# A graph attention and mixture-of-experts stack: second-layer probabilities of three target chunks made together

## The reference, cut to what matters

```
x = x + gat0(layernorm(x), adj)      # 4 heads, softmax over neighbours
x = x + moe0(layernorm(x))           # 8 experts, hidden 512, top 2
x = x + gat1(layernorm(x), adj)      # one attention matrix, see below
x = x + moe1(layernorm(x))           # 2 layers of 256x256, one of 16 experts for each run of 32 rows

gat1:  Wh = x @ W.T ; s1, s2 = score of each row and head
       z[i,j,h] = s1[i,h] + s2[j,h] ; e[i,j] = mean_h max(z, 0.2 z)
       attn = softmax(where(adj > 0, e, -inf)) ; out = attn @ Wh
```

## Time and profile before

| what | value |
|---|---|
| median of 3 runs | 751.7 us (750.96 to 751.88) |
| the profiled execution's own time | 748.28 us |
| its span, first to last instruction | 746.2 us |
| PE, DVE, ACT, POOL busy | 616.9, 532.2, 388.3, 225.4 us |
| mean granted TensorE clock | 0.903 of 2.4 GHz |
| expert weights by the SP queue (L362) | 128 transfers of 256 KB |

### The profile page before, as it was taken

One profiled execution on the slowest core, in us unless ns is written; L12 is line 12 of the kernel. 1 busy time (PEld: TensorE's weight loads), 2 busy tenths in 40 slices (PEclk: granted clock), 3 DMA queues, 4 the chain that ended last, 5 costly groups with the idle time before them and its releaser, 6 DMA issues.

```text
span 746.2 us, 14828 instructions
## 1 busy us (share of the span) xinstructions
PE 616.9 (83%) x5288; PEld 468.8 (63%) x5288; DVE 532.2 (71%) x1050; ACT 388.3 (52%) x761; POOL 225.4 (30%) x151
## 2 busy tenths in 40 slices
PE   2765466999999999989999969995479969879696
PEld 1554355687776877758777645775446737647463
DVE  6569998876687756857566289459597999998300
ACT  1876569377875778837887546541013223222231
...
DMA packets 30704, 63.09 MB, mean 85 GB/s; under 512 B 4557, under 2 KB 7637, under 8 KB 30645
## 3 DMA queue, kind: packets, MB, share of 16 engines
...
...
## 4 chain that ended last, share of the span: by engine, by line
PE 64%; DVE 17%; ACT 8%; issue 5%; POOL 3%; DMA 1%; SPq 1%; DVEq 0%; ACTq 0%
PE bank L604 16%; PE bank L616 12%; PE bank L564 10%; PE bank L687 6%; PE bank L549 5%; PE bank L724 4%; PE bank L717 3%; ACT arena L964 3%; DVE arena L1218 2%; DVE arena L1206 2%; POOL reg_b L461 2%; DVE reg_c L1360 2%; DVE arena L1214 2%; PE bank L540 1%; ACT ysb L921 1%
## 5 line engine op out<-in xcount | busy, mean ns | idle before, releaser
L454 POOL TENSOR_TENSOR x<-x,ysb 128x512 f32<-128x512 f32 x36 | 62.3, 1730 | 308.5 <-ACT ysb L921 304.2
L964 ACT ACTIVATE arena<-sbc,nd 128x512 bf16<-128x512 f32 x204 | 130.4, 718 | 37.1 <-PE bank L564 37.1
L616 PEld LDWEIGHTS bank<-arena,reg_c 128*128 128x128 f32 x1024 | 116.8, 192 | 7.2 <-issue 7.2
L604 PE MATMUL bank<-hTc,arena 128*128 128x512 f32 x256 | 120.9, 628 | 0.0
L564 PE MATMUL bank<-reg_b,arena 128*128 128x99 bf16 x2048 | 103.9, 214 | 19.6 <-DVE arena L1218 19.6
L616 PE MATMUL bank<-arena,reg_c 128*128 128x128 f32 x1024 | 116.9, 275 | 0.0
L564 PEld LDWEIGHTS bank<-reg_b,arena 128*128 128x128 bf16 x2048 | 101.4, 102 | 23.2 <-issue 11.4
L911 ACT ACTIVATE reg_c<-bank,b 128x512 f32<-128x512 f32 x128 | 87.9, 687 | 36.3 <-PE bank L604 36.3
L1206 DVE TENSOR_TENSOR arena<-maskT,arena 128x2048 bf16<-128x2048 bf16 x48 | 65.9, 1372 | 48.2 <-ACT arena L964 48.0
L1218 DVE TENSOR_TENSOR arena<-maskT,arena 128x2048 bf16<-128x2048 bf16 x64 | 95.6, 1493 | 2.2
L1360 DVE SCALAR_TENSOR_TENSOR reg_c<-reg_b,nd,reg_c 128x512 f32<-128x512 f32 x144 | 96.4, 743 | 0.0
(11 more groups left out here) (170 smaller groups left out, 795.9 us busy)
## 6 DMA issues: line engine op xcount, KB each, us to landing
arena<-in_wrT SPq DMA_DIRECT2D x128, 256.0 KB, 3.0
...
```

Source lines behind the costliest of these rows:

```text
L454: nc.gpsimd.tensor_tensor(xi, xi, ysb[:, e % 3, :].rearrange("p (t d) -> p t d", d=P), ALU.add).then_inc(s_acc, 1)
L604: mm(bank[b][:, :], w1[:, s, e % 2, c * P:(c + 1) * P], hTc[:, :], start=True, stop=True).then_inc(full[b], 1)
L616: last = mm(bank[b][:, i * P:(i + 1) * P], hid[:, e % 2, c, i * P:(i + 1) * P], w2[:, s, e % 2, c, :], start=(c == 0), stop=(c == HC - 1))
L964: last = af(ind[:, q, 1, j, :], sbc[:, h, :], ACT.Relu, bias=nd[:, q * QT + j, h:h + 1], scale=BIG)
```

## The change

The second attention no longer goes chunk by chunk. Target chunks 0, 1 and 2 are made together: one product covers WW = 1536 columns (`wide`, four slots), source tiles go in pairs (`wide_pair`, 8 products), and `attend_wide` sums a pair with 24 matmuls of 129 columns into banks 0 to 3. Five of the eight pairs are put beside the mixture of chunk 3, which keeps to banks 4 (outputs) and 5, 6, 7 (hidden blocks, HT). VectorE runs the five in a row, held only by the slots (`s_widef`: pair g waits until PE has summed pair g-2), then waits for all of GpSimd's adds of chunk 3, normalises it, and runs the other three. Chunk 3's own probabilities stay in products of 512 columns (`last_tiles`), and `attend1` sums them inside the second mixture of chunks 0, 1 and 2: 2 calls before it, then 2, 4 and 8.

For that, chunk 0 is prepared before the gate scores of chunk 3 and chunks 1 and 2 soon after, each with its source rows; the values are scaled on ScalarE (`scale_values`) instead of GpSimd; the score bounds (`nmx`) are worked out early, ahead of the first indicators; the score rows of chunk 3 go into `hT` and `ysb`, `v1` shares the buffer of `sbc`, and htt and hn of the second mixture (`tiles1`) move into the arena. The SP queue starts the selected weights after the last `attend_wide` (`full[3]`) and the scaled values. The extra indicators and source rows past the last chunk are gone, and all hardware loops but SP's are written out. `layer`, `turn`, `hidden` and `output` are as before, and so is the last chunk of the second mixture.

```diff
+WT = 3 * CT
+WW = WT * P
...
         odiv = sb("odiv", [P, CT, P])
-        sbc = sb("sbc", [P, H, CW])
+        heads = sb("heads", [P, T * (P + 1)])
+        sbc = heads[:, 0:H * CW].rearrange("p (h i) -> p h i", h=H)
+        v1 = heads[:, :].rearrange("p (t v) -> p t v", t=T)
         att = sb("att", [P, CT * 2 * VW])
...
-        whx1 = arena[:, 0:T * XM].rearrange("p (t k) -> p t k", t=T)
-        prob0 = arena[:, 4096:8192].rearrange("p (s i) -> p s i", s=8)
+        whx1 = arena[:, 0:2 * CT * XM].rearrange("p (s t k) -> p s t k", s=2, t=CT)
+        wide = arena[:, 2048:2048 + 4 * WW].rearrange("p (s i) -> p s i", s=4)
         wsel = arena[:, 0:8192].rearrange("p (s k n) -> p s k n", s=2 * L * GT, k=KC)
         at = [8192]
...
         u6 = u.rearrange("p (t h b) s v -> p t h b s v", t=T, h=H)
-        v1 = reg_b[:, 0:T * (P + 1)].rearrange("p (t v) -> p t v", t=T)
-        rows1 = reg_b[:, T * (P + 1):T * (P + 1) + 2 * H * CW]
+        rows1 = reg_b[:, 0:H * WW].rearrange("p (h i) -> p h i", h=H)
+        rows3 = [hT[:, h * CW:(h + 1) * CW] for h in range(H - 1)] + [ysb[:, 1, :]]
...
-        BANK5 = C * (E0 // 2 + 1)
+        HT = (5, 6, 7)
+        BANK3 = C + (C - 1) * E0 + 1
+        BANK5 = (C - 1) * (E0 // 2 + 1) + len(range(0, E0 * HC, len(HT))) + C
...
-                    load_pair(c, h, True)
+                    if c == C - 1 and h >= 2:
+                        sp.wait_ge(ev["y"], c * (E0 + 1) + (2 if h == 2 else 5))
+                    load_pair(c, h, c < C - 1 or h < 2)
...
-            sp.wait_ge(s_u, H + C)
-            sp.wait_ge(s_exp, 2 + C)
+            sp.wait_ge(s_v1, C)
+            sp.wait_ge(full[3], BANK3)
...
-                if c == C - 1 and e in (2, 3, 5, E0):
-                    g = (2, 3, 5, E0).index(e)
-                    tiles = slice(g * CT, (g + 1) * CT)
-                    pool.wait_ge(s_exp, 3 + g)
-                    nc.gpsimd.tensor_tensor(v1[:, tiles, 0:P], whx1[:, tiles, 0:P],
-                                            v1[:, tiles, P:P + 1].to_broadcast([P, CT, P]),
-                                            ALU.mult).then_inc(s_u, 1)
...
+            for c in range(1, C):
+                chunk0(c)
...
+            def attend_wide(g):
+                if g == 0:
+                    for b in range(WT // 3):
+                        use(b, "att")
+                pe.wait_ge(s_v1, g // 2 + 1)
+                for t in (2 * g, 2 * g + 1):
+                    pe.wait_ge(s_wide, t + 1)
+                    for i in range(WT):
+                        b, o = i // 3, i % 3 * (P + 1)
+                        last = mm(bank[b][:, o:o + P + 1], wide[:, t % 4, i * P:(i + 1) * P], v1[:, t, :],
+                                  start=(t == 0 and i % 3 == 0), stop=(t == T - 1), skip_group_check=True)
+                        if t == T - 1 and i % 3 == 2:
+                            last.then_inc(full[b], 1)
+                if g < T // 2 - 2:
+                    last.then_inc(s_widef, 1)
...
+            def first(e):
+                if e % 2 == 0:
+                    pe.wait_ge(s_wp[e // 2 % 2], k.event(f"pair{e // 2 % 2}", 32))
+                for c in range(HC):
+                    b = HT[(e * HC + c) % len(HT)]
+                    use(b, "hid")
+                    mm(bank[b][:, :], w1[:, e // 2 % 2, e % 2, c * P:(c + 1) * P], hTc[:, :], start=True,
+                       stop=True).then_inc(full[b], 1)
+            def second(e):
+                use(4, "y")
+                pe.wait_ge(ev["hid"], (C - 1) * E0 * HC + (e + 1) * HC)
+                for i in range(CT):
+                    for c in range(HC):
+                        last = mm(bank[4][:, i * P:(i + 1) * P], hid[:, e % 2, c, i * P:(i + 1) * P],
+                                  w2[:, e // 2 % 2, e % 2, c, :], start=(c == 0), stop=(c == HC - 1))
+                last.then_inc(full[4], 1)
...
+            prepare1(0)
+            source_rows1(0)
+            scores(odiv)
+            first(0)
+            first(1)
+            prepare1(1)
+            prepare1(2)
+            second(0)
+            source_rows1(1)
+            source_rows1(2)
+            first(2)
+            second(1)
+            combine(4)
+            first(3)
+            second(2)
+            first(4)
+            second(3)
+            attend_wide(0)
+            first(5)
+            second(4)
+            attend_wide(1)
+            first(6)
+            second(5)
+            attend_wide(2)
+            first(7)
+            second(6)
+            attend_wide(3)
+            second(7)
+            attend_wide(4)
             prepare1(3)
-            for q in range(2, Q):
-                quad(q)
+            source_rows1(3)
+            for g in range(5, T // 2):
+                attend_wide(g)
+            attend1(0)
+            attend1(1)
...
-                            for h in range(H):
-                                source_row(h, next_rows)
+                        for t in products.get((i, l), ()):
...
+                        for t in products.get((i, l), ()):
+                            attend1(t)
                         turn(i)
...
+            expert_chunk(odiv, {(1, 0): (2,), (2, 0): (3,)})
+            expert_chunk(xn, {(0, 0): (4,), (1, 0): (5,), (2, 0): (6,), (3, 0): (7,)})
+            expert_chunk(odiv, {(0, 0): (8,), (0, 1): (9,), (1, 0): (10,), (1, 1): (11,), (2, 0): (12,),
+                                (2, 1): (13,), (3, 0): (14,), (3, 1): (15,)})
...
+            def scale_values(c):
+                act.wait_ge(s_exp, 3 + c)
+                for i in range(CT):
+                    t = c * CT + i
+                    last = af(v1[:, t, 0:P], whx1[:, c % 2, i, 0:P], ACT.Copy, scale=v1[:, t, P:P + 1])
+                last.then_inc(s_v1, 1)
...
+            scale_values(0)
+            first(0)
+            gate()
+            first(1)
+            prepare1(1)
+            prepare1(2)
+            second_layer(0, 4)
+            source_rows1(1)
+            source_rows1(2)
+            scale_values(1)
+            scale_values(2)
+            first(2)
+            second_layer(1, 4)
+            combine(4)
+            for e in range(3, E0):
+                first(e)
+                second_layer(e - 1, 4)
+            second_layer(E0 - 1, 4)
             prepare1(3)
-            sums(3 * (P + 1), P + 1)
+            source_rows1(3)
+            scale_values(3)
+            sums(*[3 * (P + 1)] * (WT // 3), to=reg_b)
...
+            then(v.tensor_tensor(wnorm[:, 0:H], wnorm[:, 0:H], wnorm[:, H:2 * H], ALU.max))
...
+            replicate(1)
+            dve.wait_ge(s_acc, E0 + 1)
+            norm(0, 2 * C - 1)
             merge(C - 1, H - 1)
-            norm(C - 1, 2 * C - 1)
+            norm(C - 1, C, odiv)
+            dve.wait_ge(s_acc, (C - 1) * (E0 + 1))
+            statistics(CT)
+            then(statistics(2 * CT, CT))
+            deviations(2 * CT)
+            dve.wait_ge(ev["hTc"], 2 * C)
+            scale(CT, xn, 0)
             best(C - 1, 2 * C - 1)
+            dve.wait_ge(ev["hTc"], 2 * C + 1)
+            scale(2 * CT, odiv, CT)
             gate(C - 1, 2 * C - 1)
...
+            def products(h, tiles, slots, row, columns, ready):
+                before = k.at("step") - len(tiles)
+                for j, t in enumerate(tiles):
+                    p = slots[:, t % slots.shape[1], :]
+                    if h:
+                        dve.wait_ge(s_step, before + j + 1)
+                    last = v.scalar_tensor_tensor(p, row, nd[:, t, h:h + 1], p if h else maskT[:, t, columns],
+                                                  ALU.max, ALU.mult)
+                    last.then_inc(s_step if h < H - 1 else ready, 1)
+                if h < H - 1:
+                    k.event("step", len(tiles))
+            def wide_pair(g):
+                dve.wait_ge(s_exp, 3 + g // 2)
+                if g >= 2:
+                    dve.wait_ge(s_widef, g - 1)
+                for h in range(H):
+                    products(h, (2 * g, 2 * g + 1), wide, rows1[:, h, :], slice(0, WW), s_wide)
+            def last_tiles(first, n):
+                if first >= 8:
+                    dve.wait_ge(s_probf, first // QT - 1)
+                for h in range(H):
+                    products(h, range(first, first + n), prob, rows3[h], slice(WW, N), s_prob)
+            def merge1(t0, n, at, src):
+                a3 = src[:, 0:(at + n) * (P + 1)].rearrange("p (t v) -> p t v", v=P + 1)
+                for i in range(n):
+                    xo = x[:, t0 + i, :]
+                    last = v.scalar_tensor_tensor(xo, a3[:, at + i, 0:P], rden[:, at + i:at + i + 1], xo, ALU.mult,
+                                                  ALU.add)
+                return last
+            def divisors(n, src):
+                a3 = src[:, 0:n * (P + 1)].rearrange("p (t v) -> p t v", v=P + 1)
+                then(v.reciprocal(rden[:, 0:n], a3[:, 0:n, P]))
```

(26 more changed lines are left out.)

287 lines of the change are left out of this document (77 added, 210 removed).

## The result

The changed kernel takes **754.6 us** (median of 6 runs, 754.1 to 757.5) against 751.4 of the kernel before in the same comparison: 1.0051 of its time, with a 95% interval of 1.0032 to 1.0069. It is slower, by a little; the forecast of 750.4 had it 0.2% faster. The profiled execution has a span of 752.2 us (746.2 before).

What follows compares the result with a forecast made beforehand. Bounds by stretch: TensorE in chunk 3's mixture and the last chunk, VectorE's products between, both in the second mixture. 581.9 to W plus 163 gave span 744.9; adding 2.1 and 3.4 gave 750.4 us, range 739 to 764.

Steps and rivals of the forecast that it cites:

- W: Point where the last `attend_wide` is done: forecast at T + 135.6 = 581.9 us, with 163 us following to the end.
- The product of 1536 columns: VectorE's wide product: 1.73 us each, from a line through two measured sizes; a pair of tiles 13.8 us.
- Rival 4: Wide products save nothing, at 1.99 us each: 17 us, total 767; chance 0.03.
- T: Point where the twelfth score row is ready, ahead of the wide pairs: forecast at 446.3 us.
- GpSimd is kept out for the whole run: Beside VectorE's runs of products, a GpSimd add waits until the run ends: waits of 9.75, 16.44 and 22.07 us.
- rival 2: Wide products don't keep GpSimd out: pairs end at T + 71.8, W 10 us earlier, total 740.4; chance 0.12.
- The gap of 2.1 us: VectorE's wait for `attend_wide(0)` after two pairs; three GpSimd adds wait there, and the third was taken to get in.
- rival 1: GpSimd's third add misses VectorE's gap, so chunk 3 is normalised 10 us later, at T + 98: total 760; chance 0.27.
- GpSimd's adds have four outputs of slack: In the second mixture, behind W, VectorE's narrow products beside GpSimd's adds were taken to cost nothing.
- The weights: Second mixture: SP queue issues 1.15 us apart, 9.2 us a tile; last output W + 116, TensorE's path W + 118.
- Tiles and the end: Second-mixture tiles of 7.8, 8.2 or 8.6 us with no, one or two sums; 44.0 us after the last output before chunk 3.
- Rival 3: TensorE's clock holds the second mixture: 9.9 us a tile instead of 9.2, 8 us over twelve tiles, total 758; chance 0.09.

Runs made afterwards that it cites:

- experiment 1: The changed kernel with two one-hot slots, GpSimd writing the next chunk's one-hot rows right after the chunk's bias add: 746.2 us, ratio 0.9949 to the kernel before.
- experiments 8 to 14: Last sums one tile earlier, earlier first weight transfers, half-size transfers or shared register reads, on the changed kernel or experiment 1: 736.2 to 756.8 us.

## Why the prediction was wrong, point by point

The sum had two halves, up to W and behind it. Both were off, in opposite directions; the second decided.

- **The product of 1536 columns: right.** 1.73 us forecast, 1.729 measured where nothing is beside it. Rival 4 is out.
- **T: right, in part by luck.** 446.3 forecast, 446.10 measured. The last second-layer block ends at 406.0 where I had 407.1, and from there it takes 40.1 us where I had 39.2, of which 8.5 were an estimate; the two errors cancel. `attend_wide(0)` ends at T + 31.8 where I had T + 29.8, so the small latencies that I had left out of TensorE's path cost 2 us.
- **"GpSimd is kept out for the whole run": wrong for the new width.** The step took a behaviour seen at 512 columns over to 1536. It is rival 2's mechanism, to which I gave 0.12, with a price that neither had: the five pairs end at T + 77.4, not T + 73.0 (rival 2: T + 71.8), since each of eight adds costs VectorE 1.03 us. But the mixture isn't held up, and chunk 3 is normalised 5.3 us behind the pairs in the place of 15.4. The gap of 2.1 us, the third add and rival 1 had no object. Rival 2's source, the Trainium skill's "SBUF — State Buffer", Who interferes with whom, has the two engines block each other for one instruction. The eight 128x512 adds beside 1536 columns agree with it, VectorE's 1.03 us for an add of 1.27 included, which my rival 2 had left out. The adds that were held don't, for 22 to 33 us beside 512 and 768 columns and for 7.10 and 21.07 us with 128x4 beside 1536, and there the measurement decides.
- **W: 576.8 where I had 581.9** (the last wide matmul record ends there). In terms: T -0.2, pairs +4.4, the rest of chunk 3 -10.1, the last three pairs +0.8, their trailing +0.1.
- **"GpSimd's adds have four outputs of slack": the step that failed.** It counted who waits for the adds and not what is queued behind them on GpSimd: the store's issue and the one-hot copy of the next chunk, for which TensorE waits. The waits are 2.36 + 7.39 us, and experiment 1 removes them and 7.7 us of the time. Behind W 175.4 us follow, +12.4 on my 163; with the slots it is 164.3. The trace of before showed the copy 5 us ahead of its use, behind the gap that the change closes.
- **The weights: right as a limit, wrong in its sequel.** The changed kernel's TensorE loses 2.9 us to them in all, in one layer of the last chunk (3.94 us from 734.89 on, in the place of 1.02; the profile shows 0.4 of it as idling), and the kernel before loses 2.8 in the same place. The lost time at the heads gave the rest slack. I had them 2 us from being the bound; experiments 8 to 14 show that they are, once the heads are mended. That about half of their 1.15 us is the queue's register reads I had not asked.
- **Tiles and the end: right.** A tile with one sum takes 8.22 us (8.2 forecast), one with two 8.56 (8.6); from the end of the last output before chunk 3 to the end it is 44.1 (44.0). Rival 3 is out: from 624 to 662 the granted clock was 0.96, and it was low only behind the gaps at the heads.

Together: the span is 752.2 against my 744.9, 7.3 longer (-5.1 before W, +12.4 behind it). To that I had added 5.5 us for the execution's own surplus and its distance to the median; here the median is 2.4 above the profiled span, so the median missed by 4.2. That the miss is so small is luck: the mechanism that I had wrong for the wide products gave 5 us back and hid part of the loss of the step that failed.

What stays open: why a 128x512 add gets in beside 1536 columns and a 128x4 add at times doesn't, and why some adds get in beside narrow products; and what spreads the spans of one mended kernel over 4 to 6 us.
